# ScalarE weights the token's own value in the DPP attention stage of a six-stage network, instead of VectorE

## What is computed

```python
_, top_idx = jax.lax.top_k(sim, M)                      # M = 8 keys among the tokens up to i
for comb in COMBS:                                      # all sets of 1 and of 2 of the 8 slots
    idx = jnp.concatenate([jnp.full((nc, 1), i), top_idx[slots]], axis=1)
    K, V = k[idx], v[idx]                               # the token itself is always in the set
    gram = jnp.einsum('cnd,cmd->cnm', K, K)
    score = jnp.log(jnp.linalg.det(gram) + 1e-06) / (s + 1)
    w = jax.nn.softmax(K @ q_i / HS ** 0.5)             # weights inside the set
    out_s = jnp.einsum('cn,cnd->cd', w, V)
probs = jax.nn.softmax(scores)
best = jnp.argmax(probs)
y_st = outs[best]
y_soft = probs @ outs
y = y_st + stop_gradient(y_soft - y_st)                 # in value: y_soft
return jnp.where(has_valid, y, v[i])
```

## Time and profile before

| what | value |
|---|---|
| median of 3 runs | 6697.57 us (6695.38 to 6705.53) |
| profiled execution, its own time | 6691.49 us |
| its span | 6689.8 us |
| TensorE busy | 4900.3 us (73%) |
| VectorE busy | 4611.5 us (69%) |
| ScalarE busy | 2738.6 us (41%) |
| GpSimd busy | 1463.5 us (22%) |

### The profile page before, as it was taken

The page is one execution under the profiler, slowest core; times in us unless marked ns, Lnnn a source line. Parts: engine busy times, 40 slices in busy tenths (PEclk is TensorE's granted clock), DMA queues, the critical chain, the costliest instruction groups (busy, mean ns, idle before and its releaser), DMA issues. The chain is left out here.

```text
span 6689.8 us, 140956 instructions
## 1 busy us (share of the span) xinstructions
PE 4900.3 (73%) x46216; PEld 3823.2 (57%) x46217; DVE 4611.5 (69%) x9872; ACT 2738.6 (41%) x9313; POOL 1463.5 (22%) x1253
## 2 busy tenths in 40 slices
PE   5777776867877777777877788765089498419995
PEld 2333334756666666666666666655078376419995
DVE  5777774328999999999999999994168744312224
ACT  3343342214555555555555555542322133333331
POOL 1323322110000000000000000000645200266663
PEclk8777778987667777767767777765599699559997
DMA  8000000002111111211211111111222500211114
GB/s 144 8 5 7 5 3 6 0 7 78 71 68 70 72 65 72 72 69 69 72 72 66 72 71 66 72 59 29 70 70 75 109 0 10 77 61 46 46 46 138
DMA packets 226734, 370.27 MB, mean 55 GB/s; under 512 B 104818, under 2 KB 187355, under 8 KB 201028
## 3 DMA queue, kind: packets, MB, share of 16 engines
q1 hardware_dynamic: 200036, 309.26, 15.6%
q0 software_dynamic: 26112, 53.64, 2.4%
HBM read 287.04 MB, written 75.78 MB: 54 GB/s over the span
## 5 line engine op out<-in xcount | busy, mean ns | idle before, releaser
L2729 PE MATMUL l2a_g<-l2a_feat,l2a_onehot 128*128 128x33 bf16 x27648 | 782.7, 182 | 357.8 <-DVE l2a_onehot L2600 155.6
L2729 PEld LDWEIGHTS l2a_g<-l2a_feat,l2a_onehot 128*128 128x128 bf16 x27648 | 762.1, 100 | 419.0 <-issue 238.7
L2592 DVE TENSOR_REDUCE l2a_dots<-l2a_prod 128x144 f32<-128x2304 f32 x192 | 489.7, 2551 | 4.5
L1942 PE MATMUL l_y<-l_hc,l_selT 128*96 128x512 f32 x384 | 295.4, 864 | 264.9 <-POOL l_hc L1780 264.3
L2675 PE MATMUL l2a_s<-l2a_qkT 32*128 32x128 f32 (+1 forms) x1536 | 488.2, 453 | 0.0
L2701 PE MATMUL l2a_m<-main_ident,l2a_pv 128*96 128x128 f32 x2304 | 349.6, 326 | 87.7 <-DVEq L2537 87.7
L2365 POOL TENSOR_TENSOR l2a_veto<-l2a_gone 128x288 f32<-128x288 f32 x64 | 42.6, 665 | 1681.5 <-DVE l2a_prod L2585 1681.5
L2600 DVE TENSOR_SCALAR l2a_onehot<-l2a_spread,l2a_pos 128x4096 bf16<-128x4096 bf16 x288 | 361.3, 1283 | 62.3 <-DVE l2a_hd L2498 20.1
L2701 PEld LDWEIGHTS l2a_m<-main_ident,l2a_pv 128*96 128x96 f32 x2304 | 341.6, 207 | 103.5 <-issue 100.2
L1780 POOL TENSOR_TENSOR l_hc<-l_hs,l_bc 128x512 f32<-128x512 f32 x192 | 243.3, 1267 | 716.0 <-DVE l_hs L1847 714.8
L2675 PEld LDWEIGHTS l2a_s<-l2a_qkT 32*128 32x128 f32 x1536 | 310.8, 250 | 86.4 <-issue 38.6
(11 more groups left out here) (412 smaller groups left out, 11615.4 us busy)
## 6 DMA issues: line engine op xcount, KB each, us to landing
l2a_spread<-l2a_idx_rows SPq DMA_DIRECT2D x192, 1024.0 KB, 4.7
rows_in<-main_zeros SPq DMA_DIRECT2D x1, 13824.0 KB, 80.3
l2f_xg<-rows_in SPq DMA_DIRECT2D x72, 192.0 KB
l3f_xg<-rows_in SPq DMA_DIRECT2D x72, 192.0 KB, 2.5
l2f_combine_y<-rows_out SPq DMA_DIRECT2D x32, 384.0 KB, 3.8
l3f_combine_y<-rows_out SPq DMA_DIRECT2D x32, 384.0 KB, 4.7
l3f_w<-in_l3f_w SPq DMA_DIRECT2D x2, 4608.0 KB, 31.6
l_xT<-in_l_xT SPq DMA_DIRECT2D x16, 384.0 KB, 3.8
```

Source lines behind the costliest of these rows:

```text
L1942: nc.tensor.matmul(y_ps[:, :], selT[:, g, :], hc[:, g % 2, :], start=g == 0, stop=g == G - 1).then_inc(hc_used, 1)
L2592: nc.vector.tensor_reduce(dots[:, quad_of(s[2]), 0:NPROD], prod[:, :, :, :], AX.X, ALU.add).then_inc(S["dots_ready"], 1)
L2729: ins = nc.tensor.matmul(o[:, a * FEAT:a * FEAT + 2 * HS + 1], onehot[:, kt, at:at + P], feat3[:, s[1], kt, part, h, 0:2 * HS + 1], start= ...
```

## The change

The own part of the weighted sum moves from VectorE to ScalarE. VectorE now ends its round with the product over the eight slots; the sum of the weights raises a semaphore of its own, `alpha_sum`. ScalarE gets `own_values`: it forms 1 - sum for the twelve heads (`Identity`, scale -1, bias a column of ones), waits for that result, and then multiplies the kept own values with it, one instruction per head, since the weight is a column operand. `turn_output` on TensorE waits for `pv_ready` and for the new `own_part`. `keep` waits for its own copy. Beside that, `split_middle` is written ahead of the inverses.

```diff
@@ ScalarE @@
                 def keep(n, u):
 
-                    act.wait_ge(S["pv_ready"], counted(n * 2))
+                    act.wait_ge(S["own_part"], counted(n * 2))
                     for t in range(2):
                         ins = nc.scalar.copy(kept[:, t, :].rearrange("p (h d) -> p h d", h=H),
                                              feat[:, u, t, :, HS:2 * HS])
                     ins.then_inc(S["kept_ready"], 1)
+                    act.wait_ge(S["kept_ready"], counted(n + 1))
...
+                def own_values(n, u, t):
+                    r = n * 2 + t
+                    act.wait_ge(S["alpha_sum"], counted(r + 1))
+                    nc.scalar.activation(hd[:, 1, :], hd[:, 3, :], ACT.Identity, bias=one[:, :],
+                                         scale=-1.0).then_inc(S["own_weight"], 1)
+                    act.wait_ge(S["own_weight"], counted(r + 1))
+                    act.wait_ge(S["yT_psum"], counted(r))
+                    for h in range(H):
+                        ins = nc.scalar.activation(pv[:, SLOTS, h * HS:(h + 1) * HS], kept[:, t, h * HS:(h + 1) * HS],
+                                                   ACT.Copy, scale=hd[:, 1, h:h + 1])
+                    ins.then_inc(S["own_part"], 1)
...
+                    if i == 0 and in_range(n):
+                        split_middle(n, u)
                     if stage(back, LOGS):
                         inverses(*stage(back, LOGS))
                     if i == 0 and back(1):
                         keep(back(1)[0], back(1)[1])
-                    if i == 0 and in_range(n):
-                        split_middle(n, u)
...
                     if stage(back, WEIGH):
+                        own_values(*stage(back, WEIGH))
                         turned(*stage(back, WEIGH))
@@ VectorE, weigh_stage @@
-                    send(nc.vector.tensor_reduce(hd[:, 3, :], alpha[:, :, :], AX.X, ALU.add))
+                    nc.vector.tensor_reduce(hd[:, 3, :], alpha[:, :, :], AX.X, ALU.add).then_inc(S["alpha_sum"], 1)
                     dve.wait_ge(S["yT_psum"], counted(r))
                     link(TT(pv[:, 0:SLOTS, :].rearrange("p a (h d) -> p h a d", h=H), values[:, t, :, :, 0:HS],
                             alpha[:, :, :].unsqueeze(3).broadcast_to([P, H, SLOTS, HS]), ALU.mult))
-                    link(nc.vector.tensor_scalar(hd[:, 3, :], hd[:, 3, :], -1.0, 1.0, ALU.mult, ALU.add))
-                    dve.wait_ge(S["kept_ready"], counted(n + 1))
-                    link(TT(pv[:, SLOTS, :].rearrange("p (h d) -> p h d", h=H),
-                            kept[:, t, :].rearrange("p (h d) -> p h d", h=H), over(hd[:, 3, :], HS), ALU.mult))
                     dve.sem_inc(S["pv_ready"], 1)
@@ TensorE, turn_output @@
                     pe.wait_ge(S["pv_ready"], counted(n * 2 + t + 1))
+                    pe.wait_ge(S["own_part"], counted(n * 2 + t + 1))
```

More of the change, by code:

```diff
@@ L2077, in dpp_attention_phase @@
         alpha = m.sb("alpha", [P, H, SLOTS])
+        one = m.sb("one", [P, 1])
         hd = m.sb("hd", [P, 5, H])
@@ L2098, in dpp_attention_phase @@
             det_ready kept_ready pv_ready yT_psum yT_ready proj_ready x_added veto_ready own_chain first_chain
-            second_chain third_chain minus_ready quarter_ready dve_held act_held pe_held pool_held sp_held""".split()
+            second_chain third_chain minus_ready alpha_sum own_weight own_part quarter_ready dve_held act_held pe_held pool_held sp_held""".split()
         S = {name: m.sem(name) for name in names}
@@ L2181, in _ @@
                 for name in "xn_ready a_sb mid_ready idxT_ready kv_ready log_ready exp_ready inv_ready probs_ready " \
-                            "kept_ready yT_ready squared extended minus_ready quarter_ready placed".split():
+                            "kept_ready yT_ready squared extended minus_ready quarter_ready placed own_weight " \
+                            "own_part".split():
                     act.sem_inc(S[name], 1)
@@ L2409, in _ @@
             def _(dve):
-                for name in ("own_ready scored idx_found marked onehot_ready dots_ready bent_ready diff_ready "
+                for name in ("alpha_sum own_ready scored idx_found marked onehot_ready dots_ready bent_ready diff_ready "
                              "det_ready denom_ready most_ready pv_ready x_added").split():
@@ L2423, in _ @@
                 nc.vector.memset(dots[:, :, :], 0.0)
+                nc.vector.memset(one[:, :], 1.0)
                 nc.vector.memset(veto[:, :, :, :], -1e30)
@@ L2504, in weigh_stage @@
                     r = n * 2 + t
-                    chain, link, send, tt = chained("third_chain", 17, r)
+                    chain, link, send, tt = chained("third_chain", 14, r)
                     TT = nc.vector.tensor_tensor
```

## The result

The change makes the kernel slower: 6902.2 us median (6891.0 to 6904.5, 4 runs) against 6696.7 us before (6695.4 to 6705.5, 4 runs), ratio 1.030 (95% interval 1.028 to 1.032). The direction and the place were forecast, the size was not: 118 us were forecast, 205 measured, and 6902 lies above the range.

The account below looks back on a forecast made before the run. VectorE was taken to carry the stage, with a TensorE-ScalarE path as long once per image; 3.1 + 1.5 - 0.6 = 4.0 us in 30 images (+120), less 2, gave +118 on the 6697.6 median: 6815 us, range 6733 to 6880.

Parts of the forecast that it names:

- The saving on VectorE: Two instructions removed from VectorE's round: 0.69 us saved with t = 0, 0.60 with t = 1.
- The price of `own_values`: On ScalarE: twelve products at 0.20 us a step, 2.49 us; 2.76 us from ScalarE free to TensorE released.
- The order argument: With t = 0, own_values stands behind ScalarE's copy of the third front unit, so turn_output starts 3.8 us later.
- The serial path to the logarithms: From turn_output with t = 0 through TensorE and ScalarE to L2494: a 3.8 us delay lengthens the stage, less any slack.
- The faster rival: Work goes from a full engine to a half empty one and nothing else happens: 6656 us, chance 0.06.
- 3.1 us (delay): Mean cost per image of the later turn_output: 3.8 us in 12 images of 28, 2.6 in the other 16.
- 1.5 (clock): Cost per image from the clock on the delayed path: 1.5 us, taken between 0 and 2.7.
- 0.6 (t = 1): With t = 1 the later TensorE start costs nothing, so VectorE's saving of 0.60 us is won.
- the much slower rival: Step of 0.31 us and whole path behind the wait at half clock, over 2.7 us an image: above 6890 us, chance 0.05.
- the upper bound: Most the clock term could cost per image: 2.7 us.
- The row I called nearest: The profile row of 6.84 us, cited for taking the clock term above the middle of its range.
- The slack: Room before VectorE needs the logarithms at L2494: 1.17 us, from one image, applied to 16 of 28 images.

Follow-up runs that it names:

- experiment 2: Changed kernel with own_values of t = 0 placed behind front unit 0 instead of front unit 2 in ScalarE's program: 6702.0 us, ratio 0.9998.
- experiment 3: Changed kernel with TensorE's turning starting on the eight slots, waiting for the own part only before its last two products (output wrong): 6705.8 us, ratio 1.0004.
- experiment 5: Changed kernel with 16 further TensorE products of pv ahead of the wait for the own part, t = 0 only: 6808.7 us, ratio 1.017.
- experiment 4: Changed kernel with the own part on ScalarE for t = 1 only, VectorE making it for t = 0 as before: 6705.3 us, ratio 1.0002.
- experiment 10: Changed kernel with the own part on ScalarE for t = 0 only, VectorE making it for t = 1 as before: 6904.0 us, ratio 1.031.
- experiment 1: Changed kernel with split_middle put back behind the inverses and keep, own part still on ScalarE: 6904.3 us, ratio 1.030.
- experiment 7: Kernel before the change, with the twelve logarithms of the t = 1 round moved on ScalarE from step 3 to step 2: 6657.8 us, ratio 0.994.
- experiment 8: Changed kernel with the edits of experiment 2 and experiment 7 together: 6622.0 us, ratio 0.989.

## Why the prediction was wrong

What held, with its numbers. The saving on VectorE (0.68 us with t = 0, as costed). The price of `own_values`: twelve products of 294 ns in 2.49 us, exactly the forecast, and 2.81 us from ScalarE's copy to the turning for 2.76 (3108.41 to 3111.22 in the image shown). The order argument: the turning stands behind ScalarE's copy of front unit 2. The serial path to the logarithms and the wait at its end. Not foreseen was the second wait on it, for the gather: with 150.9 us it is the largest of VectorE, where the forecast expected the one for the logarithms to be. The faster rival is refuted as it was set up, and for the reason given: experiments 2 and 3 take the delay away and the loss goes.

The step that failed is the size of three terms of the sum, 3.1 us (delay) + 1.5 (clock) - 0.6 (t = 1) = 4.0 us an image forecast and 6.8 measured. Over 30 images, counted from VectorE's product with t = 0: the turning starts 5.0 us later (6.59 to 11.58), takes 2.7 us longer (4.10 to 6.82), the path behind it to the end of the logarithms is 0.1 us longer (17.45 to 17.51), 0.4 us of slack ahead of L2494 are used up, and from there to the next product an image is 0.7 us shorter. 5.0 + 2.7 + 0.1 - 0.4 - 0.7 = 6.7 us; in the 28 steady images it is 6.8. The time came out above 6890, where the much slower rival stood with its chance of 0.05, but not by that rival's way: the step was 0.20 us and not 0.31, and the clock took no more than the 2.7 us of the upper bound.

**The clock, 1.5 us.** The upper bound of 2.7 us is 6.84 - 4.10, at granted clocks of 0.54 and 1.00. That less than all of it would be paid was my estimate, and no run shows the 1.5 us; the runs show 2.7. Over 30 images the turning takes 6.82 us for 4.10, so 2.7, and from the end of the gather to the logarithms' end the path is as long as before (3120.5 to 3135.58 in the image shown, 15.1 us; 1985.39 to 2000.44 before, 15.1 us). Nothing was given back on this path. In experiment 5 the turning takes 4.14 us again, which confirms the size. The row I called nearest was simply the answer.

**"The 0.60 us are won", t = 1.** They are not: experiment 4 has the gain alone and is no faster, experiment 10 lacks it and is no slower. My argument looked for new waits of VectorE in steps 4 and 5 and found none, rightly. It missed that a shorter VectorE has to find the other path shorter too when it comes to L2494. In experiment 4 0.57 of the 0.60 us come back there, in experiment 2 all 1.29. In the sum above the 0.6 us are within the 0.7; yet experiment 10, which lacks them, has the same length of an image, as its turning starts 0.2 us sooner after the product (11.34) and takes 0.1 us less (6.69).

**The mean delay, 3.1 us.** It was 5.0 - 0.4 = 4.6 us. Two parts. The slack was taken from one image, 1.17 us in 16 of 28, 0.67 in the mean; over 30 images it is 0.41 in the mean, so less could be covered. And TensorE reaches the turning later, measured from VectorE's product: over 30 images ScalarE's copy of unit 2 ends 8.66 us after it, 7.62 before. With 2.92 us from there to the turning, its start moves from 6.59 to 11.58 us, by 5.0 instead of 3.8. Why the copy comes 1.0 us later is open; in experiment 10, where VectorE keeps its work with t = 1, it still comes 0.8 us later (8.42).

**Why a shorter VectorE gains nothing** is the more useful question. The length of an image is the same, to 0.02 us, in kernels whose VectorE has up to 1.3 us less to do (taken one image later, from the fourth to the thirty-second, the first four lie between 93.83 and 93.92):

| kernels | us per image |
|---|---|
| before, experiments 2, 3, 4 | 93.89, 93.88, 93.89, 93.88 |
| change, experiments 1, 10 | 100.69, 100.69, 100.69 |
| experiment 7 / experiment 8 | 92.43 / 91.07 |

In the first two lines a path over TensorE ends last, in the third VectorE. What may hold such a path at one length shows in two kernels that I set to the same start, the end of the wait at the first instruction of `log_stage` in one image (3126.72 in the kernel before, 3128.61 in experiment 4). The next image but one, TensorE, kernel before:

```profile
3287.80 5.72 PE L2648 MATMUL l2a_a<-l2a_tT,l2a_wqk 96*96 96x256 f32 x16 [0.67 <-ACT l2a_tT L2211]
3293.35 4.09 PE L2701 MATMUL l2a_m<-main_ident,l2a_pv 128*96 128x128 f32 x36
```

and experiment 4:

```profile
3288.95 6.41 PE L2676 MATMUL l2a_a<-l2a_tT,l2a_wqk 96*96 96x256 f32 x16 [0.67 <-ACT l2a_tT L2213]
3295.20 4.09 PE L2731 MATMUL l2a_m<-main_ident,l2a_pv 128*96 128x128 f32 x36
```

The front units start 161.08 us after the common point in the one and 160.34 in the other, 0.74 us earlier. They take 0.69 us longer, and the turning starts at 166.63 and 166.59. The granted clock in these stretches is 0.64 and 0.56:

```profile
3287.80:3293.50 5.70, 5.70 (x18) 4.04 (x19) 5.36 (x6) 0.83 (x2) 0.00 (x0) 0.64 0.51 183
```

```profile
3288.95:3295.30 6.35, 6.35 (x17) 4.38 (x18) 6.32 (x6) 0.83 (x2) 0.00 (x0) 0.56 0.48 165
```

The granted clock goes from 0.50 to 1.00 at 3291.93 in the kernel before and at 3294.49 in experiment 4:

```profile
3290.93:3291.93 1.00, 1.00 (x4) 0.71 (x3) 1.00 (x3) 0.36 (x1) 0.00 (x0) 0.50 0.64 262
3291.93:3292.93 1.00, 1.00 (x7) 0.74 (x6) 0.96 (x2) 0.47 (x2) 0.00 (x0) 1.00 1.16 475
```

```profile
3293.49:3294.49 1.00, 1.00 (x4) 0.69 (x3) 1.00 (x1) 0.06 (x1) 0.00 (x0) 0.50 0.47 197
3294.49:3295.49 1.00, 1.00 (x7) 0.78 (x6) 1.00 (x3) 0.09 (x1) 0.00 (x0) 1.00 0.00 0
```

That is 165.21 and 165.88 us after the common point. The work began 0.74 us earlier, but the change to 1.00 came 0.67 us later, so that what was gained was spent at a granted clock of 0.50. The equal lengths and this pair are shown. That the clock's rises hold every such path at its length, in all images, is argued from them and was not tested by itself; nor does it explain why the front units start later relative to VectorE in some images than in others.

## What to carry to other kernels

Before work is moved off a full engine, ask which engine's program the result is waited for in, and what stands ahead of it there: here 2.8 us on a half idle ScalarE became 5.0 us on TensorE's queue, and 2.7 more through its clock. The idle time to look for is that ahead of the new instruction's place, not behind it; one line in another place took back all 205 us. And where a full engine waits even a little for a path over the others, shorten that path first (an image became 1.5 us shorter here, 0.5 of it the wait): only then was relief of the full engine worth anything (0.98 of 1.29 us). And look at which engines work beside the full one, since a new order can change how long its instructions take (here one took 1.02 us in the mean beside GpSimd and 0.55 without it).

## What was not expected of the hardware

- Filling TensorE's wait with useless products made the program 93 us faster (6902 to 6809 us), for the most part through the granted clock of 1.00 for 0.59 behind it.
- A path over TensorE kept its length to 0.02 us per image over four kernels, and to 0.01 over three. In the one pair of images laid side by side its work began 0.7 us earlier and took 0.7 us longer, at a granted clock of 0.56 for 0.64.
- A start of TensorE's turning 1.9 us later cost 1.4 us an image, one 2.2 us sooner won 3.5 (100.69 to 97.18): delays did not add, as the turning itself took 0.9 us less in the first (5.93 for 6.82) and 1.1 us less in the second.
- An instruction of VectorE that takes 0.55 us alone took 1.02 in the mean, and up to 1.21, when GpSimd worked beside it (L2516, 28 of 56 runs each).
